# A gated linear attention block: the sums over the key index with stationary matrices of 32 columns

## The reference, cut to what matters

```
def step(S, inp):
    qt, kt, vt, ft = inp
    S = jnp.exp(ft)[..., None, None] * S + kt[..., :, None] * vt[..., None, :]
    o = jnp.einsum('bhk,bhkv->bhv', qt, S)
    return (S, o)
...
o = o * gate
mu = jnp.mean(o, axis=-1, keepdims=True)
xc = o - mu
var = jnp.mean(xc * xc, axis=-1, keepdims=True)
o = xc / jnp.sqrt(var + EPS_LN) * ln_w
return o @ Wo.T
```

## Time and profile before

| what | value |
|---|---|
| median of three executions | 573.6 us |
| the profiled execution | 576.63 us, of it 574.8 us span |
| mean granted TensorE clock | 0.851 of full |
| TensorE matmul busy | 422.7 us (74%) |
| VectorE busy | 368.3 us (64%) |
| GpSimd busy | 293.0 us (51%) |
| ScalarE busy | 197.8 us (34%) |
| line 517 matmuls (the reduces) | 74.2 us of modelled duration in all |

### The profile page before, as it was taken

The page is one execution under the profiler, slowest core; times in us unless marked ns, Lnnn a source line. Parts: engine busy times, 40 slices in busy tenths (PEclk is TensorE's granted clock), DMA queues, the critical chain, the costliest instruction groups (busy, mean ns, idle before and its releaser), DMA issues. The chain is left out here.

```text
span 574.8 us, 8665 instructions
## 1 busy us (share of the span) xinstructions
PE 422.7 (74%) x2116; PEld 324.1 (56%) x2117; DVE 368.3 (64%) x1037; ACT 197.8 (34%) x502; POOL 293.0 (51%) x330
## 2 busy tenths in 40 slices
PE   4671476787999999999998566656888888889200
PEld 4441234455787786868675365544677767767200
DVE  4459837978879899898998406331455545555185
ACT  3350240322626354543322212201434444444160
POOL 0124154362565847575765415260456566666553
PEclk9665778795989999998999857769989999999755
DMA  9600000000000000000000000032022222221393
GB/s 264 267 1 0 0 1 1 0 2 1 1 32 6 29 9 20 19 9 25 10 29 5 23 15 28 9 83 47 20 70 76 69 73 73 69 74 56 90 287 92
DMA packets 32965, 28.57 MB, mean 50 GB/s; under 512 B 4362, under 2 KB 29970, under 8 KB 32658
## 3 DMA queue, kind: packets, MB, share of 16 engines
q1 hardware_dynamic: 28578, 19.20, 11.9%
q0 software_dynamic: 4352, 8.95, 4.7%
HBM read 17.10 MB, written 12.10 MB: 51 GB/s over the span
## 5 line engine op out<-in xcount | busy, mean ns | idle before, releaser
L1025 POOL TENSOR_TENSOR qS<-S,qT 128x512 f32<-128x512 f32 x56 | 72.0, 1286 | 59.7 <-PE obank L517 44.9
L1115 POOL DMA_INDIRECT y_dram<-S x72 | 71.0, 987 | 15.6 <-issue 10.4
L1042 POOL DMA_INDIRECT h_dram<-h,target_i x64 | 63.8, 997 | 15.8 <-issue 14.6
L1492 DVE COPY qS<-ff 128x256 f32<-128x256 f32 x72 | 30.5, 424 | 61.9 <-PE ff L731 55.0
L506 PE MATMUL at<-vT_hi,spread_v 128*128 128x512 f32 x64 | 47.2, 737 | 28.9 <-DVE S L1246 28.9
L517 PE MATMUL obank<-qS,gather_v 128*128 128x512 f32 x112 | 65.0, 673 | 2.7 <-POOL qS L1025 2.5
L1233 DVE TENSOR_TENSOR at<-at,khat 128x512 f32<-128x512 f32 x64 | 43.5, 689 | 17.2 <-PE at L507 16.7
L608 PE MATMUL ff<-w_gain,work 128*128 128x128 f32 x256 | 36.6, 312 | 9.3 <-issue 7.7
L608 PEld LDWEIGHTS ff<-w_gain,work 128*128 128x128 f32 x256 | 36.4, 228 | 10.4 <-issue 7.8
L722 PE MATMUL ff<-w_hi,vT_lo 128*128 x72 | 35.2, 489 | 9.4 <-DVE vT_lo L1478 7.7
L973 ACT ACTIVATE S<-ff 128x256 f32<-128x256 f32 x72 | 27.6, 384 | 39.9 <-PE ff L724 25.9
(11 more groups left out here) (189 smaller groups left out, 1065.8 us busy)
## 6 DMA issues: line engine op xcount, KB each, us to landing
S<-h_dram SPq DMA_DIRECT2D x72, 64.5 KB
work<-in_w13T SPq DMA_DIRECT2D x1, 2560.0 KB, 9.9
xall<-in_x SPq DMA_DIRECT2D x8, 256.0 KB, 5.4
w_hi<-y_dram SPq DMA_DIRECT2D x8, 256.0 KB, 4.8
w_lo<-y_dram SPq DMA_DIRECT2D x8, 256.0 KB, 5.4
out<-work SPq DMA_DIRECT2D x8, 256.0 KB, 2.3
w_sb<-in_w2T SPq DMA_DIRECT2D x1, 1280.0 KB, 12.5
y_dram<-S POOLq DMA_INDIRECT x72
```

What stands on the lines that cost most here:

```text
L1025: pool.tensor_tensor(qS[:, v % 2, :], S[:, v, :], qT[:, b % 2, :], ALU.mult).then_inc(s_qS, 1)
L1042: pool.indirect_dma_start(out=h_dram[:, :], out_offset=bass.IndirectOffsetOnAxis(ap=target_i[:, k, t:t + 1], axis=0), in_=h2[:, k, t, :], ...
L1115: pool.indirect_dma_start(out=y_dram[:, :], out_offset=bass.IndirectOffsetOnAxis(ap=rows[:, u, P:P + 1].bitcast(I32), axis=0), in_=y_sb[:, ...
L1492: dve.tensor_copy(t_GT[:, u % RING, :], ff[2 + u % 2][:, 0:HID]).then_inc(s_tGT, 1)
```

## The change

The eight matmuls with stationary matrices of 128 columns become eight with 32 columns, in two sets of four. Within a set, each of the four has its own quadrant of the output's partitions (columns 0, 32, 64 and 96 of the array, `tile_position`), and its own product. Half of the 32 columns are zero: the first set (value indices 0 to 3) fills the first 16 columns of each quadrant, the second set (4 to 7) the last 16, and adds to the first. The output's features are thereby in another order, and the gate's weights, Wo and ln_w are permuted on the host to match. qS grows from a ring of two to a ring of four; s_red counts 2 per block. A set waits for its last product.

```
-            def reduce(b, v):
-                if v == 0:
+            def gather(b, k):
+                if k == 0:
                     wait(pe, s_og, b)
-                if v < HD - 1:
-                    wait(pe, s_qS, (HD - 1) * b + v + 1)
+                    wait(pe, s_qS, (HD - 1) * b + HD // 2)
                 else:
+                    wait(pe, s_qS, (HD - 1) * (b + 1))
                     wait(pe, s_q7, b + 1)
-                product = qS[:, v % 2, :] if v < HD - 1 else khat[:, b % 2, :]
-                pe.matmul(obank[:, :], gather_v[:, v, :], product, start=(v == 0), stop=(v == HD - 1)).then_inc(s_red, 1)
+                for n in range(HD // 2):
+                    product = qS[:, n, :] if k == 0 or n < HD // 2 - 1 else khat[:, b % 2, :]
+                    ins = pe.matmul(obank[n * NQ:(n + 1) * NQ, :], gather_v[:, k, :], product, start=(k == 0), stop=(k == 1),
+                                    tile_position=(0, n * NQ))
+                ins.then_inc(s_red, 1)
...
             def period(i):
                 on(spread, i, 0)
-                on(reduce, i - 1, 4)
-                on(reduce, i - 1, 5)
                 on(up, i - 3, 2)
                 on(project, i + 1, 0)
-                on(reduce, i - 1, 6)
                 on(spread, i, 1)
                 on(project, i + 1, 1)
-                on(reduce, i - 1, 7)
+                on(gather, i - 1, 1)
                 on(spread, i, 2)
...
                 on(spread, i, 3)
-                on(reduce, i, 0)
                 on(spread, i, 4)
...
-                on(reduce, i, 1)
                 on(spread, i, 6)
...
                 on(project, i + 1, 4)
-                on(reduce, i, 2)
+                on(gather, i, 0)
                 on(positions, i - 2)
                 on(spread, i, 7)
                 on(transpose_rn, i + 1)
                 on(up, i - 2, 1)
-                on(reduce, i, 3)
...
             def drain():
                 a, b, c = NB - 3, NB - 2, NB - 1
-                reduce(c, 4)
-                reduce(c, 5)
                 up(a, 2)
                 transpose_x2(b, c)
-                reduce(c, 6)
                 logits(b)
-                reduce(c, 7)
+                gather(c, 1)
                 transpose_back(b)
...
             def query(b, v):
                 wait(pool, s_scan[half(v)], scans(b, v))
-                wait(pool, s_red, HD * b + (v - 1 if v != 1 else -2))
+                wait(pool, s_red, 2 * b + v // (HD // 2))
...
-            for v in range(HD):
-                dve.tensor_copy(gather_v[:, v, :].rearrange("p (h k) -> p h k", k=HD)[:, :, v],
-                                gather_src(block_diag, ident, v, H, HD))
+            for k in range(2):
+                dve.tensor_copy(gather_v[:, k, k * H:(k + 1) * H], head_ones[:, :])
...
             def gate_o(b):
-                wait(dve, s_red, HD * b + HD)
+                wait(dve, s_red, 2 * b + 2)
...
             def normalise_k(b):
                 wait(dve, s_rnT, b + 1)
-                wait(dve, s_red, HD * (b - 1))
+                wait(dve, s_red, 2 * (b - 1))
...
+def gathered_order(H, HD):
+    return [h * HD + half * (HD // 2) + n for n in range(HD // 2) for half in range(2) for h in range(H)]
```

More of the change, by code:

```diff
@@ L99, in build @@
     ROW = P + 1
+    NQ = 2 * H
+    assert NQ * HD // 2 == P
     assert D == P and NC == 2 and NEXP == 8 and NSH == 2 and HD == 8 and N % TB == 0
@@ L123, in build @@
         consts_sb = sb("consts_sb", list(consts.shape))
-        ident, head_ones, block_diag, center, before, ones, mean_col, rank, keep, region = \
-            parts(consts_sb, P, H, P, P, P, P, 1, NEXP, NB, NEXP)
+        ident, head_ones, center, before, ones, mean_col, rank, keep, region = \
+            parts(consts_sb, P, H, P, P, P, 1, NEXP, NB, NEXP)
         ids_sb = sb("ids_sb", [P, 2, NB * NT], I32)
@@ L132, in build @@
         spread_v = sb("spread_v", [P, HD, P], F32R)
-        gather_v = sb("gather_v", [P, HD, P])
+        gather_v = sb("gather_v", [P, 2, NQ])
         cmod_sb = sb("cmod_sb", [P, B + 6 * P])
@@ L186, in build @@
         S = sb("S", [P, HD, TB])
-        qS = sb("qS", [P, 2, TB])
+        qS = sb("qS", [P, HD // 2, TB])
         og = sb("og", [P, TB])
@@ L238, in build @@
         t_G = decay[:, :, :].rearrange("p a (r n) -> p (a r) n", n=HID)
-        t_GT = qS[:, :, :].rearrange("p a (r n) -> p (a r) n", n=HID)
+        t_GT = qS[:, 0:2, :].rearrange("p a (r n) -> p (a r) n", n=HID)
         t_hi, t_lo = (a[:, :].rearrange("p (r n) -> p r n", n=P) for a in (vT_hi, vT_lo))
@@ L1021, in query @@
                 wait(pool, s_scan[half(v)], scans(b, v))
-                wait(pool, s_red, HD * b + (v - 1 if v != 1 else -2))
+                wait(pool, s_red, 2 * b + v // (HD // 2))
                 if v == 0:
                     wait(pool, s_act, 5 * b + 5)
-                pool.tensor_tensor(qS[:, v % 2, :], S[:, v, :], qT[:, b % 2, :], ALU.mult).then_inc(s_qS, 1)
+                pool.tensor_tensor(qS[:, v % (HD // 2), :], S[:, v, :], qT[:, b % 2, :], ALU.mult).then_inc(s_qS, 1)
             def add_shared(b):
@@ L1525, in _ @@
             add_x(NB - 1)
-def gather_src(block_diag, ident, v, H, HD):
-    return block_diag[:, :].rearrange("p (h k) -> p h k", k=HD)[:, :, v]
+def gathered_order(H, HD):
+    return [h * HD + half * (HD // 2) + n for n in range(HD // 2) for half in range(2) for h in range(H)]
 def constants(H, HD, NEXP, NB, BPB):
@@ L1540, in constants @@
         p[:, None] // HD == np.arange(H)[None, :],
-        p[:, None] // HD == p[None, :] // HD,
         np.eye(P) - 1.0 / P,
@@ L1579 @@
     NC = HID // P
+    order = gathered_order(H, D // H)
     w1 = np.concatenate([np.asarray(L0_ffn_sw1), np.asarray(L0_ffn_w1)])
@@ L1589 @@
         "cmod": np.concatenate([np.asarray(L0_c).T, np.asarray(L0_wmod)], axis=1),
-        "attw": np.concatenate([np.asarray(w).T for w in (L0_attn_Wq, L0_attn_Wk, L0_attn_Wv, L0_attn_Wf, L0_attn_Wo)]
-                               + [np.asarray(L0_attn_ln_w).reshape(D, 1), np.asarray(L0_ffn_router_w).T], axis=1),
-        "wg12": np.concatenate([np.asarray(L0_attn_Wg1), np.asarray(L0_attn_Wg2).T], axis=1),
+        "attw": np.concatenate([np.asarray(w).T for w in (L0_attn_Wq, L0_attn_Wk, L0_attn_Wv, L0_attn_Wf)]
+                               + [np.asarray(L0_attn_Wo).T[order], np.asarray(L0_attn_ln_w).reshape(D, 1)[order], np.asarray(L0_ffn_router_w).T], axis=1),
+        "wg12": np.concatenate([np.asarray(L0_attn_Wg1), np.asarray(L0_attn_Wg2).T[:, order]], axis=1),
         "w13T": w13.transpose(3, 0, 1, 2).reshape(D, NFF, 2 * HID),
```

## The result

The changed kernel takes 584.37 us, the median of four executions from 581.95 to 586.07; the kernel before, on the same chip beside it, 573.37. The ratio is 1.0193 with a 95% interval of 1.0149 to 1.0237: slower by 11 us, where 572.8 was forecast and the range of 560 to 587 was given. The profiled execution took 583.83 us (span 582.0), so the two traces differ by 7.2 us; the kernel before's profiled execution stood 3 us above its own median, and that part of the 11 us can't be read from the traces.

A forecast was written before the change was run, and what follows sets the result against it. TensorE and VectorE were both taken to be near their limit. Steady periods +3.2, periods 0 to 2 -5.6 and drain +1.6 gave -0.8 us on the profiled 576.63, taken off the median 572.8 us; range 560 to 587.

The forecast's parts named there:

- the step on GpSimd: Steady periods: `query(i, 0)` starts about 3 us later, hidden by 4.84 us idle before `split_h2`; vanished reduce waits free nobody else.
- GpSimd becomes the bound: Rival, chance 0.04: the 3 us shift is not absorbed by GpSimd's idle time; about 1 us a period, 579 us.
- the rival without overlap: Rival, chance 0.28: no matmuls of a set run side by side; set 3.44 us, +10.5 us, or 584.
- The prediction's own sign of being wrong: Forecast wrong if VectorE's wait before `gate_o` falls, or the 31.8 us block at full clock changes by over 1.5 us.
- A set, 2.15 us: Four reduce calls on TensorE half overlap: 5 x 0.43 = 2.15 us, between 0.86 and 3.44.
- `gate_o` 1.05 us later, five blocks: Behind `spread(i, 1)` the whole second set replaces the eighth reduce, delaying `gate_o` in five blocks from 156.6 us: +5.2 us.
- The router's wait goes: Middle of steady blocks: reduces leave the stretch before `logits`, removing VectorE's 1.6 us wait before the router's choice.
- Steady blocks +3.2: Five blocks from 156.6 us: +5.2 for later `gate_o`, against 1.6 of router's wait and 0.4 of small waits.
- Periods 0 to 2, -5.6: Early periods, clock often half: reduces and their waits leave places where VectorE waits for TensorE; together -5.6 us.
- Drain +1.6: Chain to the end: the set in place of the eighth reduce adds 1.3 us, a slower clock start 0.3.
- The clock, "up to +4, not in the sum": Steady periods: less busy TensorE may have two or three more clock drops of 1.2 to 1.7 us each.
- Full overlap gives 561.6: Rival, chance 0.28: four quadrants run together, set 0.86 us, `gate_o` 0.25 us earlier in five periods; -12.0 us.

The follow-up runs named there:

- seven buffers: The changed kernel with seven buffers for qS in place of four, so no query waits for a set of its own block: 569.78 us, ratio 0.9947.
- fillers: The changed kernel with added matmul calls of zero columns only where TensorE idled, four a block from the third, three at the drain's start: 575.33 us, ratio 1.0035.
- short reduces: The kernel before with the reduces of value indices 1 to 7 streaming 8 of the 512 tokens: 577.11 us, ratio 1.0029.

## Why the prediction was wrong

Its sign failed in the step on GpSimd: "`query(i, 0)` now waits for the second set, about 3 us later than before", "so this is hidden", and "Its waits for reduces within a block go, and free nobody else." The first wait was foreseen with about its size (12.3 us in five blocks, 2.5 each), and so was the idle time that swallows it; GpSimd's busy time a block is nearly unchanged and it never became the bound. The second was not foreseen: `query(i, 4)` waits for the whole first set, 10.5 us in the five blocks and 3.6 at the longest. The term of both was put at nothing. With it taken away by seven buffers the kernel is about 14 us faster by ratio. What was not looked at is what a shifted query runs beside. The rows for it were in the prediction's own hands: in period 0 it read that VectorE's small operations took 1.18 us instead of 0.16 while GpSimd worked, counted a gain for the one place where the overlap goes away, and did not ask where the shift would make new ones. The rival "GpSimd becomes the bound" had the right engine, 579 us and a chance of 0.04, by another mechanism. That 584.37 lies in the range, at the 584 of the rival without overlap, is chance: that rival's set of 3.44 us isn't there. The prediction's own sign of being wrong, a block of 31.8 us that changes by more than 1.5, came true.

- **A set, 2.15 us**: mis-sized. It is 0.99: the first halves of all four calls run together, and then the second halves.
- **`gate_o` 1.05 us later, five blocks**: it comes 2.46 us behind `last_query` instead of 2.52, and this term is zero. In the second to fourth block the clamp is yet 0.4 us later and the instruction behind it up to 0.75; 0.1 of this is TensorE's, and the rest stays open. TensorE's idle time ahead of `spread(i, 1)` was forecast at 2 to 3 us a block; it is 5.3 us in five.
- **The router's wait goes**: right, 1.6 to 0.7 us over the three periods, the rest of it at the low clock.
- **Steady blocks +3.2**: +8.4, all of it in two blocks: 4.2 in the third (0.8 in line 74, 2.6 at the low clock, the rest around the clamp) and 4.4 in the last (3.0 in stretched instructions, 1.4 in waits), less 0.3 in the others. With the ring of seven the same blocks are 2.8 us shorter than before.
- **Periods 0 to 2, -5.6**: -4.3 at the third `last_query`. The sum is near, its parts are not: up to the second `last_query` -3.1 was forecast and it is -5.6, and period 2, forecast at -2.5, is 1.35 us longer. There `gate_o` comes 0.94 us later behind `last_query`, at a clock of 0.77 in this stretch.
- **Drain +1.6**: +3.5 to `project_out`. The slower start was named and priced at 0.3; it is 2.
- **The clock, "up to +4, not in the sum"**: it came, in one block by 2.6 us, in the drain by 2, and in period 2, where fillers give back 3.9. It was left out of the sum though the earlier trace rows showed the half clock behind an idle stretch of 3 us, and the change makes such stretches.
- **Full overlap gives 561.6**: this rival had the set right and the time wrong by 23 us. It lacked the same term for the queries, and it took TensorE's saved time ahead of `gate_o` as the kernel's. The short reduces (ratio 1.0029) gained nothing by such time.

Shown: the waits of the queries cost about 14 us by ratio in the changed kernel (seven buffers), and without GpSimd's long queries the loss is gone. Shown for the clock: 2 us of the drain, and 3.9 us between the second and the third `last_query` that fillers give back. Only argued: how the rest parts between stalls, late queries and the clock that falls behind them. Fillers alone also gave back 9 us by ratio, 3.4 of them in a part of the trace that they don't touch, and the short reduces lost 4.8 us in the five blocks without any of the new waits.

## What to carry to other kernels

When a change moves a wait of GpSimd, list what VectorE runs in the new place, and not only whether GpSimd has room: each instruction with two inputs in SBUF can be held for a query's length. Then follow who waits for it: a stretched instruction cost nothing where a wait behind it became shorter, and 4 to 5 us where TensorE went idle behind it and its clock fell. A ring that is released in sets makes its first user wait for the whole set; buy the buffers together with the batching. Time taken from a fully busy engine counts only where the one that bounds the end waits for it.

## What of the hardware was not expected

- Four float32 calls of 32 columns on four quadrants take 0.99 us for all eight matmuls, a single one of them (two matmuls) 0.98: the second halves overlap as the first do.
- A change between 128 and 32 columns costs 0.1 to 0.2 us on each side, little enough at two sets a block, and enough to make single narrow calls slower than wide ones.
- A VectorE instruction of 0.16 us took 1.95, more than GpSimd's query of 1.28. It began in a scatter's issue, 0.63 us before the recorded start of the query that follows directly, and ended with the query. Scatters without a query so near behind them held none of these instructions.
- Zero matmuls at the places of the old reduces, on TensorE's path, raised the mean clock from 0.822 to 0.881 without a gain. Three of them in the idle gap of the drain raised its start from 0.50 to 0.77, with a gain of 2 us.
- The same instructions in front of the drain gave one block at a low clock in one trace and two, others, in another.
